# Adding a mixture of experts' routed rows into the output: by a last pass over them, or by the scatter that carries them

## The reference

```python
scores = softmax(xt @ gate_w.T)                    # 2048 tokens, 8 experts
_, idx = top_k(scores + gate_b, 2)
weights = take_along_axis(scores, idx)             # two weights per token
comb = (weights[..., None] * one_hot(idx, 8)).sum(1)
for each expert e:                                 # D = 256, I = 512
    h = swiglu((xt @ w1[e] + b1[e]) * (xt @ w3[e] + b3[e]))
    routed += comb[:, e:e+1] * (h @ w2[e] + b2[e])
shared = swiglu((xt @ sw1 + sb1) * (xt @ sw3 + sb3)) @ sw2 + sb2
return x + routed + shared                         # x: the input of this layer
```

## Time and profile before

| | |
|---|---|
| time, median of 3 runs | 948.82 us (946.68 to 951.16) |
| profiled execution | 949.27 us, its span 947.5 us |
| mean granted TensorE clock | 0.98 |
| busy, share of the span | PE 93%, DVE 67%, ACT 56%, POOL 41% |
| DMA | 154 MB, mean 163 GB/s |
| chain that ended last, by engine | PE 62%, DVE 16%, DMA 7%, ACT 6%, issue 5%, POOL 3% |

### The profile page before, as it was taken

The page is one execution under the profiler, slowest core; times in us unless marked ns, Lnnn a source line. Parts: engine busy times, 40 slices in busy tenths (PEclk is TensorE's granted clock), DMA queues, the critical chain, the costliest instruction groups (busy, mean ns, idle before and its releaser), DMA issues.

```text
span 947.5 us, 14991 instructions
## 1 busy us (share of the span) xinstructions
PE 880.6 (93%) x4301; PEld 614.2 (65%) x4302; DVE 635.4 (67%) x1269; ACT 529.9 (56%) x847; POOL 387.9 (41%) x334
## 2 busy tenths in 40 slices
PE   8987789889999999999999999899999999999992
PEld 4644455545555545555457887778888887888881
DVE  4798987855557457456488788846666666566666
ACT  2548885445665665765554434326666665566650
POOL 2134455425676746756514546512222222222210
PEclk9999999989999999999999999999999999999996
DMA  9400000009469478568475100078711298326405
GB/s 307 103 1 1 0 1 1 1 15 365 168 254 342 173 294 331 203 264 343 192 260 202 69 1 1 12 303 335 300 37 39 81 356 340 161 74 265 105 26 178
DMA packets 49909, 154.07 MB, mean 163 GB/s; under 512 B 6266, under 2 KB 24438, under 8 KB 44236
## 3 DMA queue, kind: packets, MB, share of 16 engines
q1 hardware_dynamic: 46124, 144.25, 40.5%
q0 software_dynamic: 3744, 9.31, 3.2%
HBM read 97.85 MB, written 56.62 MB: 163 GB/s over the span
## 4 chain that ended last, share of the span: by engine, by line
PE 62%; DVE 16%; DMA 7%; ACT 6%; issue 5%; POOL 3%; SPq 1%; DVEq 0%; ACTq 0%; POOLq 0%
PE banks L1043 11%; PE banks L1294 6%; PE banks L1296 6%; PE banks L1295 6%; PE banks L1012 3%; DMA aux<-moe_x,small 3%; PE banks L1035 3%; PE banks L1036 3%; PE banks L950 2%; DMA wsplit<-cv_hl 2%; PE banks L1331 2%; PE banks L1332 2%; PE banks L1333 2%; PE banks L1307 1%; PE banks L916 1%
## 5 line engine op out<-in xcount | busy, mean ns | idle before, releaser
L1043 PE MATMUL banks<-wexp 128*65 128x512 f32 (+1 forms) x288 | 150.1, 602 | 3.8 <-ACT wexp L1601 3.8
L673 POOL TENSOR_TENSOR cv_hl<-wexp,cv_hl 128x1024 fp32r<-128x1024 f32 x45 | 108.5, 2417 | 57.4 <-ACT cv_hl L1578 56.8
L1294 PE MATMUL banks<-ring,x_hi 128*128 x312 | 128.0, 410 | 0.0
L1296 PE MATMUL banks<-ring,x_lo 128*128 x312 | 122.9, 394 | 0.0
L1295 PE MATMUL banks<-ring,x_hi 128*128 x312 | 122.6, 393 | 0.0
L1601 ACT ACTIVATE wexp<-banks 128x512 f32<-128x512 f32 x128 | 76.2, 598 | 72.1 <-PE banks L1036 71.8
L2081 DVE TENSOR_REDUCE small<-banks 128x1 bf16<-128x1101 f32 x64 | 83.6, 1307 | 39.2 <-PE banks L1012 39.2
L1737 ACT ACTIVATE banks<-wexp 128x1024 f32 x72 | 73.4, 1020 | 47.7 <-DVE aux L2462 47.7
L1715 ACT ACTIVATE aux<-banks 128x512 f32<-128x512 f32 x78 | 46.6, 597 | 64.5 <-PE banks L1296 48.3
L1035 PE MATMUL banks<-q_hi,k_hl 128*128 128x512 f32 x144 | 75.7, 525 | 1.7 <-ACT q_lo L1569 1.0
L745 POOL DMA_INDIRECT moe_y<-aux,small x20 | 20.6, 1030 | 116.4 <-DVE aux L2472 116.4
(11 more groups left out here) (374 smaller groups left out, 2192.2 us busy)
## 6 DMA issues: line engine op xcount, KB each, us to landing
wsplit<-cv_hl SPq DMA_DIRECT2D x45, 1024.0 KB, 8.0
ring<-wsplit SPq DMA_DIRECT2D x32, 1280.0 KB
wexp<-in_L_ffn_w SPq DMA_DIRECT2D x40, 512.0 KB, 5.9
wexp<-in_expert_biases SPq DMA_DIRECT2D x8, 1152.0 KB, 6.5
ring<-wsplit SPq DMA_DIRECT2D x4, 1024.0 KB, 8.2
wexp<-moe_y SPq DMA_DIRECT2D x7, 512.0 KB, 5.9
wexp<-in_L_ffn_sw SPq DMA_DIRECT2D x5, 512.0 KB, 9.5
x_sb<-in_x SPq DMA_DIRECT2D x4, 512.0 KB, 8.2
```

Of the source, the lines that this page charges most:

```text
L673: g.tensor_tensor(sides(hl[:, PIECE:2 * PIECE]), raw, sides(hl[:, 0:PIECE]).bitcast(f32), ALU.subtract).then_inc(s['cv_lo'], 1)
L1043: mm(pb[5 + half][0:DA, :], vh[b][0:w, c, :], pT[q % 3][0:w, :], start=c == 0, stop=c == len(KTILES) - 1).then_inc(s['a_pv'], 1)
L1294: mm(o[:], x_hi[u][:, kc, :], hi, start=kc == 0 and not primed, stop=False, skip_group_check=primed)
L1296: last = mm(o[:], x_lo[u][:, kc, :], hi, start=False, stop=primed and kc == KC - 1, skip_group_check=primed)
```

## The change

The routed result is multiplied by its row's weight as it leaves PSUM, and the scatter adds it to the output in DRAM. For this the weights go to DRAM (`row_w`, one 4-byte word for each token and choice) after the routing, and POOL gathers a column of 128 of them per slot by the row numbers (`weigh`). The output, with the shared part, is stored from `x_sb` once `result_sh` has added it (`keep_rows`). As both of a token's rows go to the same row of the output, each scatter waits until the one before it has landed. Row numbers of the output are the old ones less 2048 where they are not below it (`out_row`, three instructions behind the release of POOL). `moe_y`, the reloads, the sums, the last stores and `last_tiles` are gone. On VectorE `slots` is cut in three pieces with places of their own, and `ring_rows` stands one gate step earlier.

```diff
-        moe_y = nc.dram_tensor("moe_y", (TOPK * T * P, D), f32, kind="Internal").ap()
+        row_w = nc.dram_tensor("row_w", (TOPK * T * P, 1), f32, kind="Internal").ap()
...
 @@ SP
             arrived(1)
+            def keep_rows(t, n):
+                sp.wait_ge(s['y_add'], t + n)
+                sp.dma_start(rows_out[t * P:(t + n) * P, :].rearrange("(t p) d -> p t d", p=P), x_sb[:, t:t + n, :]).then_inc(c_out, 16)
+
+            sp.wait_ge(s['r_hot'], 1)
+            sp.dma_start(row_w.rearrange("(c t p) n -> p c (t n)", c=TOPK, p=P), route[:, 2:2 + TOPK, :]).then_inc(s['w_out'], 16)
             sp.wait_ge(s['r_slot'], 1)
+            keep_rows(0, 12)
             sp.wait_ge(s['y_full'], T)
             biases(1, 'ld_bias1')
+            keep_rows(12, 4)
             for i in (2, 3):
                 biases(i, f'ld_w{i % WRING}')
                 expert(i)
...
-            for k in range(4):
-                sp.dma_start(sum_a[:, 4 * k:4 * k + 4, :], rows_of(moe_y, 4 * k, 4)).then_inc(f_a[k], 16)
...
-            for k, (t, n) in enumerate(LAST_PIECES):
-                sp.dma_start(sum_b[:, t:t + n, :], rows_of(moe_y, t, n, 1)).then_inc(f_b[k], 16)
-            for k, (t, n) in enumerate(LAST_PIECES):
-                sp.wait_ge(s['f_add'], k + 1)
-                sp.dma_start(rows_of(rows_out, t, n), x_sb[:, t:t + n, :]).then_inc(c_out, 16)
-            sp.wait_ge(c_out, 16 * len(LAST_PIECES))
+            sp.wait_ge(c_out, 16 * 2)
...
 @@ POOL
+            def weigh(t):
+                if t < 2:
+                    pool.wait_ge(s['w_out'], 16)
+                else:
+                    pool.wait_ge(m_w[t % 2], 16 * (t // 2))
+                g.indirect_dma_start(out=slot_weight[:, t:t + 1], out_offset=None, in_=row_w,
+                                     in_offset=bass.IndirectOffsetOnAxis(ap=meta[:, 0, t:t + 1], axis=0),
+                                     bounds_check=TOPK * T * P - 1, oob_is_err=False).then_inc(m_w[t % 2], 16)
+
             def spread(t):
                 pool.wait_ge(m['ysb'], t + 3)
-                g.indirect_dma_start(out=moe_y, out_offset=bass.IndirectOffsetOnAxis(ap=meta[:, 0, t:t + 1], axis=0),
-                                     in_=y_sb[t % 2], in_offset=None,
-                                     bounds_check=TOPK * T * P - 1, oob_is_err=False).then_inc(c_scat[t % 2], 16)
+                if t == 0:
+                    pool.wait_ge(c_out, 16 * 2)
+                else:
+                    pool.wait_ge(c_scat[(t - 1) % 2], 16 * ((t + 1) // 2))
+                g.indirect_dma_start(out=rows_out, out_offset=bass.IndirectOffsetOnAxis(ap=out_row[:, t:t + 1], axis=0),
+                                     in_=y_sb[t % 2], in_offset=None, compute_op=ALU.add,
+                                     bounds_check=T * P - 1, oob_is_err=False).then_inc(c_scat[t % 2], 16)
...
             gated(4 * IC - 1)
-            for t in (1, 2):
-                fetch(t)
+            fetch(1)
+            link(g.memset(slot_weight, 0.0))
+            for t in range(2):
+                weigh(t)
+            fetch(2)
             for t in range(SLOTS):
+                if t + 2 < SLOTS:
+                    weigh(t + 2)
                 if t + 3 < SLOTS:
                     fetch(t + 3)
                 spread(t)
...
 @@ VectorE
                 v.tensor_scalar(meta[:, 1, :], meta[:, 0, :], T * P - 1, None, ALU.bitwise_and).then_inc(s['r_meta'], 1)
+                link(v.tensor_scalar(none, dest, float(T * P), -float(T * P), ALU.is_ge, ALU.mult))
+                link(v.tensor_tensor(dest, dest, none, ALU.add))
+                v.tensor_copy(out_row, dest)
...
             slot_experts()
+            ring_rows()
             gate_sh(10)
-            ring_rows()
...
             rows_of_places(0, 0)
+            bias_slots()
             line_sh(12)
             rows_of_places(0, 1)
             gate_sh(13)
             rows_of_places(1, 0)
+            weight_slots()
             line_sh(13)
             rows_of_places(1, 1)
             ve.sem_inc(s['r_hot'], 1)
             gate_sh(14)
             result_sh(1, (0, 1))
+            line_sh(14)
             slots()
-            line_sh(14)
             result_sh(1, (2, 3))
             indices()
             gate_sh(15)
             line_sh(15)
             product_sh(4 * IC - 1)
-            last_tiles()
             low_sh(4 * IC - 1)
...
             def result(t, u, turn):
                 ve.wait_ge(m['y'], t + 2)
-                if turn is not None:
+                if turn is None:
+                    ve.wait_ge(m_w[u], 16)
+                else:
+                    ve.wait_ge(m_w[u], turn * 16 + 16)
                     ve.wait_ge(c_scat[u], turn * 16)
-                v.tensor_copy(paired(y_sb[u]), sides(pb[6 + u][:, 0:D])).then_inc(m['ysb'], 1)
+                v.tensor_scalar(paired(y_sb[u]), sides(pb[6 + u][:, 0:D]), slot_weight[:, bass.ds(t, 1)], None, ALU.mult).then_inc(m['ysb'], 1)
...
-                return v.scalar_tensor_tensor(x_t, part[:, t, :], route[:, 2 + c, t:t + 1], x_t, ALU.mult, ALU.add)
```

More of the change, by code:

```diff
@@ L297, in program @@
         meta = small[:, 404:404 + 2 * SLOTS].bitcast(i32).rearrange("p (a b) -> p a b", a=2)
-        sum_a, sum_b = (wexp[:, n * WSP:n * WSP + T * D].rearrange("p (a b) -> p a b", a=T) for n in (0, 2))
+        slot_weight = small[:, 488:488 + SLOTS]
+        out_row = small[:, 528:528 + SLOTS].bitcast(i32)
+        assert TOPK == 2
         score, biased, val, row, rank, *chosen = (rt.take(T * E, T) for _ in range(5 + TOPK))
@@ L321, in program @@
         row_hot = [b.rearrange("p a b -> p (a b)").bitcast(bf16).rearrange("p (t n) -> p t n", t=T) for b in (big1, big2)]
-        last_n = rt.take(4)
-        slot_i = sb("slot_i", [1, 3 * SLOTS + E + 2], i32)
-        AT_SLOT, READY, AT_BIAS, ENDS, FIRST_DONE = 0, SLOTS, 2 * SLOTS, 3 * SLOTS, 3 * SLOTS + E
+        slot_i = sb("slot_i", [1, 3 * SLOTS + E], i32)
+        AT_SLOT, READY, AT_BIAS, ENDS = 0, SLOTS, 2 * SLOTS, 3 * SLOTS
         hot = sb("hot", [96, SLOTS], bf16)
@@ L336, in program @@
             h_up h_lift h_read h_gate h_line h_sig h_sg h_fP h_plus h_hi h_loP y_full y_add
-            xst0 xst1 f_add ld_sh ld_sh2
+            xst0 xst1 w_out ld_sh ld_sh2
             """.split()
@@ L343, in program @@
         c_scat = [sem(f"c_scat{u}") for u in range(2)]
-        LAST_PIECES = ((0, 2), (2, 4), (6, 4), (10, 4), (14, 2))
-        f_a = [sem(f"end_a{k}") for k in range(4)]
-        f_b = [sem(f"end_b{k}") for k in range(len(LAST_PIECES))]
+        m_w = [sem(f"m_w{u}") for u in range(2)]
         cv_in = [sem(f"cv_in{u}") for u in range(CVRAW)]
@@ L554, in _ @@
                 arrived(i)
[L556 to L561, removed]
-            for k in range(4):
-                sp.dma_start(sum_a[:, 4 * k:4 * k + 4, :], rows_of(moe_y, 4 * k, 4)).then_inc(f_a[k], 16)
-            for u in range(2):
-                sp.wait_ge(c_scat[u], 16 * len(range(u, SLOTS, 2)))
-            for k, (t, n) in enumerate(LAST_PIECES):
-                sp.dma_start(sum_b[:, t:t + n, :], rows_of(moe_y, t, n, 1)).then_inc(f_b[k], 16)
-            for k, (t, n) in enumerate(LAST_PIECES):
-                sp.wait_ge(s['f_add'], k + 1)
-                sp.dma_start(rows_of(rows_out, t, n), x_sb[:, t:t + n, :]).then_inc(c_out, 16)
-            sp.wait_ge(c_out, 16 * len(LAST_PIECES))
+            sp.wait_ge(c_out, 16 * 2)
         @block.gpsimd
@@ L2361, in ring_rows, with bias_slots, weight_slots @@
                 link(v.tensor_tensor(r, n, r, ALU.subtract))
-            def slots():
+            def bias_slots():
                 n, r, w = (x[0:1, :] for x in (slot_n, slot_r, slot_w))
                 link(v.tensor_scalar(w, r, float(NB), float(BRING - NB), ALU.mult, ALU.add))
-                v.tensor_copy(slot_i[:, AT_BIAS:AT_BIAS + SLOTS], w)
+                v.tensor_scalar(tend_n[0:1, :], tend[0:1, :], 1.0, None, ALU.add)
+                v.tensor_scalar(n, n, 1.0, None, ALU.add)
+                link(v.tensor_copy(slot_i[:, AT_BIAS:AT_BIAS + SLOTS], w))
+            def weight_slots():
+                r, w = (x[0:1, :] for x in (slot_r, slot_w))
                 link(v.tensor_scalar(r, r, 1.0, None, ALU.add))
@@ L2370, in slots @@
                 link(v.tensor_tensor(r, r, w, ALU.add))
+            def slots():
+                n, r = (x[0:1, :] for x in (slot_n, slot_r))
                 link(v.tensor_scalar(r, r, float(WSP), None, ALU.mult))
-                link(v.tensor_scalar(n, n, 1.0, None, ALU.add))
-                link(v.tensor_scalar(tend_n[0:1, :], tend[0:1, :], 1.0, None, ALU.add))
                 v.tensor_copy(slot_i[:, AT_SLOT:AT_SLOT + SLOTS], r)
@@ L2492, in _ @@
             result(SLOTS - 1, (SLOTS - 1) % 2, (SLOTS - 1) // 2)
-            def summed(c, t, part):
-                x_t = x_sb[:, t, :]
-                return v.scalar_tensor_tensor(x_t, part[:, t, :], route[:, 2 + c, t:t + 1], x_t, ALU.mult, ALU.add)
```

(10 more changed lines are left out.)

9 lines of the change are left out of this document (removed).

## The result

The change makes the kernel slower. The median is 967.93 us (965.70 to 976.23), that of the kernel before beside it 948.48 us; the ratio is 1.0234 (95% interval 1.0193 to 1.0274). The forecast was 942.6 us in a range of 934 to 957, so the sign is wrong and the time lies outside the range. The profiled execution took 965.70 us, its span is 964.0 us.

The account below looks back on a forecast made before the run. TensorE, busy for 93% of the span, was taken as the bound, so the output path counts only where it waits or has ended. -13.3 - 3.0 + 7.9 + 1.7 = -6.7 us on 949.27 gave 942.6 us, range 934 to 957.

Parts of the forecast that it names:

- Step 1: End of kernel: reloads, sums and stores go, the span ending soon after the last adding scatter lands: -13.3 us.
- Step 2: End of the shared stage: small VectorE instructions are spread, TensorE's idle shrinks and its clock holds: -3.0 us.
- Step 3: Routed stage: the weight gather sends each fetch out 1.32 us later, paid once for each of six loads: +7.9 us.
- Step 4: TensorE's clock in the routed stage: one more fall to half clock after the new stalls: +1.7 us (0 to +8.5).
- rival B: TensorE's clock falls at every weight load: 949.4 us, no change; chance 0.20.
- Step 5: POOL in the routed stage: each scatter's wait for the previous one's landing holds nothing up: 0 us.
- rival C: Adding scatters land slowly and POOL's serial wait sets the tiles' pace, deciding from about 7.8 us: 973 us; chance 0.10.
- Step 6: Row weights' way through DRAM: 4,096 small writes land between 609 and 616, in time: 0 us, up to +6.
- rival E: Row weights land late, at 626 instead of 620, and stall the second tile by 6 us: 948.6 us; chance 0.10.
- Step 7: The rest: the 2 MB store ahead of expert loads and the multiplying copy out of PSUM cost 0, or 0.1 us.
- Rival D: Routed stage: the later fetch costs nothing, as a stalled tile shifts the next fetches out of the load: 933.0 us; chance 0.10.

Follow-up runs that it names:

- e12: Kernel before with only the slots' small operations split in three and moved, and ring_rows one gate step earlier: 947.18 us, 0.9976.
- e7: Control: kernel before with only its two register waits written in another form: 948.76 us, 1.0012.
- e11: Kernel before with every fetch one tile earlier and each expert's weights in 16 pieces, not 4: 942.37 us, 0.9931.
- e13: Kernel before with each expert's weights loaded in 16 pieces, not 4: 944.55 us, 0.9981.
- e3: Changed kernel with a scatter that replaces the output's rows instead of adding to them: 940.44 us, 0.9934.
- e8: Changed kernel without the per-slot gather of row weights, all weights 1: 965.8 us, 1.0174.
- e4: Changed kernel without the wait for the previous scatter, each slot adding into its own row of an unread tensor: 970.13 us, 1.0212.
- e5: Changed kernel with every token fetch issued one tile earlier: 940.78 us, 0.9926.
- e1: Control: changed kernel with only its two register waits written in another form: 966.31 us, 1.0195.
- e9: Changed kernel with each expert's weights in 16 transfers of 320 KB, not 4 of 1,280 KB: 949.89 us, 1.0017.
- e6: Kernel before with every token fetch issued one tile earlier: 942.56 us, 0.9928.
- e10: Changed kernel with every fetch one tile earlier and each expert's weights in 16 pieces, not 4: 934.86 us, 0.9862.
- e14: Changed kernel with weights in 16 pieces and without the gathers of row weights, all weights 1: 944.47 us, 0.9971.

## Why the prediction was wrong, point by point

*Step 1, the tail (-13.3): right in kind, 2.5 us too large.* It brought -10.8. Behind the last issue 5.0 us remain (959.01 to 964.0), not 4.0. And the sentence "the scatter before it ... has landed by then" failed: an adding scatter takes 4.28 us with the queue empty (taken: 3.6), so the last one waits for it and goes out 1.6 us later than the copy allows.

*Step 2, the shared stage (-3.0): mis-sized.* The stage became 0.8 us shorter in the changed kernel; e12 says 0.1 to 4.5 us. The step allowed for one slow small operation and there were four; the clock still fell, at 591.5, after the pause of 1.87 us. And the step's 1.7 us for a clock that holds was not to be had: in e7, e11 and e13, with the output path and the order of the kernel before, the same pause of 2.35 us was not followed by half clock, and from the pause of 0.89 us to the first turn of tokens they took 40.4 us where the kernel before took 40.7. TensorE then waited 1.06 us for VectorE instead.

*Step 3, the fetches (+7.9): this step failed.* "Every fetch goes out 1.32 us later" was true of the gather and left out the adding scatter, which costs POOL 0.70 us more at each issue and stands in the same queue ahead of the fetch. The room fell to 4.30 us, not 5.17, and the landing rose to 8.0 to 9.0 us, not 6.9: +21.3 us over six loads where +7.9 stood. The prediction bounded the price of an adding scatter only where it is the last transfer, in the tail and against POOL's serial wait; nobody was charged for standing behind it. "So it is paid about once per load" was right. e3 gives the size: 26 us for the adding, 21.6 of them in the routed stage, clock included. The gather, the one term that the step did price, was not far off: 6.6 us more of pauses behind a plain scatter (e3 against the kernel before), about 5 us behind an adding one (e8).

*Step 4, the clock (+1.7): the mechanism held, the count didn't.* Every pause of the changed routed stage was 3.45 us or longer, and half clock came with every one: five falls more than before, not one. The routed stage's 32.1 less 21.3 us leave 10.8 us, mostly this; TensorE's busy time there, up by 10.2 us, says the same. That is somewhat above the step's upper bound (+8.5), and it is rival B's premise. B's own sum, 949.4 us, still had 1.32 us per stall. The Trainium skill, TensorE: Matmul & The Clock Gate, "HAM oscillation", has a wait for a DMA that slows the clock paid at every repetition; with these pauses the trace agrees.

*Step 5, the serial wait (0): right in this kernel* (e4), though the landing beside loads, 9.3 to 9.8 us, is past the 7.8 us from which rival C was to decide. The fetch was late before the wait could be. It decided in e5, where the fetch was no longer late. C's time of 973 us came near 967.9 by accident.

*Step 6, the row weights (0): right in effect, too short in size.* They were issued at 592.79 and landed at about 611.6, just before the first gather at 612.43; TensorE never waited for it, and rival E didn't happen. But the 18.8 us of their way (17.0 in e1 and e9) are more than the 12 to 17 that the step had worked out. Counted in the kernel before, 4.1 us later, the landing would be at 615.7, the very end of the 609 to 616. The time that the prediction, beside the Trainium skill, DMA: Bandwidth & Descriptors, "Specifications", allowed for small writes, up to 6 us, was needed in part, and the slack took it.

*Step 7 (0): right.* The copy that multiplies takes 0.49 us, not 0.44, and no pause in TensorE comes from the store of 2 MB. Rival D, that the later fetch costs nothing, was the furthest from the result.

By the steps as measured: -10.8 - 0.8 + 21.3 + 10.8 = +20.5 us, and -4.1 us of an earlier start that belongs to the execution: +16.4, against 16.5 between the two spans. That it closes proves nothing about the clock, whose 10.8 us are the remainder of the routed stage.

## What to carry to other kernels

When a transfer changes its kind, price it for those that stand behind it in its queue as well as for those that wait for its data: measure from the issue of the transfer ahead to the landing of the one that is needed, and compare that with the time until the need. A part's worth found by taking it away alone can grow once its neighbour is cured (the gather: about 5, then 11 us of the routed stage), so don't add up single prices. Read such a removal by stages too, since the time of the whole kernel showed 0.5 and 5.4 us for it, with another 4.5 us lost at the end. A wait that looks like the cause may be hidden behind another, so test it by removal. When short transfers run beside a bulk load, try the load in smaller pieces and the short ones a step earlier before giving up an otherwise sound change: the two together turned 2% slower into 1.4% faster.

## What the runs showed of the hardware that was not expected

- An indirect scatter that adds took POOL 1.6 to 1.7 us to issue (plain: 1.02), landed after 4.3 to 4.7 us on an empty queue (plain: 2.36), after 9.3 to 9.8 us beside a weight load of 1,280 KB pieces (8.0 to 10.6 in e5; plain, in e3: 6.7 to 7.0), and after 7.3 to 8.7 us beside one of 320 KB pieces.
- 320 KB pieces instead of 1,280 KB let POOL's transfers beside the load land 1 to 3 us sooner, and from the load at about 670 us on SP spent 9.7 to 11.3 us on the 16 issues instead of 2.1 on the four, with no loss that the runs show (e11 against e6: 942.4 and 942.6 us). 160 KB pieces gave nothing more.
- The length of a pause alone doesn't tell whether TensorE's clock falls: the one of 1.86 us at 593 us was followed by half clock in e9 and not in e10, two kernels that differ only in the fetches' lead, and the one of 2.35 us near 603 us in the kernel before, but not in e7, e11 and e13.
- 4,096 stores of 4 bytes, in one transfer, landed 17.0 to 18.8 us after their issue (e1, e9 and the kernel after).
- In both kernels without the gather (e8, e14) the span goes on for 9.6 us after the last scatter's issue, not 4.9 to 5.0 us; it is a drain at the end of POOL's program, and its cause is open.
